# One-hot rows of 19 of 32 slot groups moved from ScalarE and VectorE to GpSimd

## What is computed

```python
x = x + _L0_xattn_ref(_layernorm(x), ctx_768, Wq, bq, Wk, bk, Wv, bv, Wo, bo)
x = x + _L0_ffn_ref(_layernorm(x), expert_embeddings, first_linear, second_linear)

# _L0_ffn_ref, the part that matters here
weights = _router(x, expert_embeddings)           # softmax over the top 2 of 8 experts
cap_ones = where(cumsum(ones, axis=0) <= 1024, ones, 0)
vals, idx = top_k((weights * cap_ones).T, 1024)   # per expert: which tokens it takes
tokens = x_flat[idx]
inter = relu(einsum('ech,eih->eci', tokens, first_linear))
out = einsum('eci,ehi->ech', inter, second_linear) * vals[:, :, None]
final = zeros.at[idx].add(out)
```

## Time and profile before

| | us |
|---|---|
| median of 3 runs | 1480.37 |
| lowest, highest | 1473.51, 1483.36 |
| the profiled execution | 1479.05 |
| its span, first to last instruction | 1477.3 |

### The profile page before, as it was taken

How to read it: one execution, slowest core, us unless ns; L and a number is a source line. 1 busy time by engine, 2 the same in 40 slices (tenths; PEclk the granted TensorE clock), 3 DMA queues, 4 the chain that set the end, 5 groups by cost and what they waited for, 6 DMA issues and landing times.

```text
span 1477.3 us, 30732 instructions
## 1 busy us (share of the span) xinstructions
PE 1338.2 (91%) x12330; PEld 786.1 (53%) x12330; DVE 997.5 (68%) x1998; ACT 814.1 (55%) x1344; POOL 702.3 (48%) x655
## 2 busy tenths in 40 slices
PE   7446999989999899997765999999999999999996
PEld 3334777766677667765444544444444444444442
DVE  6686888899889998899874644555454544555431
ACT  3556888877999889987554333425151433425110
POOL 2155877777777767776412424251413324251301
PEclk9767999999999999999787999999999999999998
DMA  7336798878878667786713665464646565474401
GB/s 220 101 92 136 191 228 216 216 175 208 196 210 193 176 157 177 186 216 146 197 61 116 180 157 158 131 178 119 182 136 157 159 160 163 132 169 118 105 15 43
DMA packets 321160, 231.78 MB, mean 157 GB/s; under 512 B 253481, under 2 KB 253865, under 8 KB 321018
## 3 DMA queue, kind: packets, MB, share of 16 engines
q1 hardware_dynamic: 305658, 179.17, 48.2%
q0 software_dynamic: 15360, 50.66, 11.5%
HBM read 121.87 MB, written 50.86 MB: 117 GB/s over the span
## 4 chain that ended last, share of the span: by engine, by line
PE 71%; DVE 16%; issue 4%; POOL 3%; ACT 3%; DMA 1%; SPq 1%; DVEq 0%; POOLq 0%; ACTq 0%
PE ps L1178 22%; PE ps L1164 22%; PE ps L1064 8%; PE ps L994 6%; PE ps L1045 4%; DVE ps L1409 2%; PE ps L1081 2%; PE ps L979 2%; DVE sd L1422 2%; DVE sm L1443 2%; DVE x L1465 1%; PE ps L1017 1%; PE ps L1059 1%; DVE xnT L1402 1%; PE ps L968 1%
## 5 line engine op out<-in xcount | busy, mean ns | idle before, releaser
L1164 PE MATMUL ps<-xT,w1s 128*128 128x512 f16 (+1 forms) x1632 | 335.9, 368 | 6.2 <-DVE xT L1708 5.4
L1178 PE MATMUL ps<-w2s,hT 128*128 128x512 f16 x1536 | 332.8, 379 | 0.0
L821 ACT ACTIVATE hT<-ps 128x512 f16<-128x512 f32 (+1 forms) x136 | 77.8, 572 | 359.6 <-PE ps L1164 359.6
L1164 PEld LDWEIGHTS ps<-xT,w1s 128*128 128x128 f16 x1632 | 160.4, 98 | 179.5 <-issue 5.8
L1178 PEld LDWEIGHTS ps<-w2s,hT 128*128 128x128 f16 x1536 | 150.3, 98 | 181.2
L994 PE MATMUL ps<-xnT,wqh 128*128 128x256 f16 x1536 | 202.1, 285 | 20.1 <-ACT partq L704 19.9
L542 POOL TENSOR_TENSOR sd<-sd,rr 128x1232 f32<-128x1232 f32 x64 | 144.2, 2253 | 145.6 <-ACT rr L722 145.6
L579 POOL DMA_INDIRECT out_dram<-ys,idx x64 | 71.7, 1120 | 278.4 <-DVE ys L1748 278.4
L1738 DVE SCALAR_TENSOR_TENSOR hT<-ps,hT 128x512 f16<-128x512 f32 (+1 forms) x136 | 88.6, 658 | 138.0 <-ACT hT L821 137.8
L1064 PE MATMUL ps<-woh,oT 128*128 128x512 f16 x768 | 179.9, 384 | 0.7 <-POOL oT L530 0.7
L994 PEld LDWEIGHTS ps<-xnT,wqh 128*128 128x128 f16 x1536 | 154.3, 102 | 47.7 <-ACT partq L704 21.5
(11 more groups left out here) (203 smaller groups left out, 2016.8 us busy)
## 6 DMA issues: line engine op xcount, KB each, us to landing
xt<-x SPq DMA_DIRECT2D x64, 256.0 KB, 3.4
xr<-x SPq DMA_DIRECT2D x64, 256.0 KB, 3.8
xrow_dram<-x SPq DMA_DIRECT2D x64, 256.0 KB, 3.7
out_dram<-x SPq DMA_DIRECT2D x64, 256.0 KB, 4.1
stage<-w1T SPq DMA_DIRECT2D x8, 2048.0 KB, 9.9
stage<-w2T SPq DMA_DIRECT2D x8, 2048.0 KB, 8.4
xs<-x SPq DMA_DIRECT2D x62, 256.0 KB, 3.9
wqf<-wq SPq DMA_DIRECT2D x1, 1024.0 KB, 7.1
```

The lines of the kernel that those rows point to most:

```text
L1164: ins = pe.matmul(hb[z][:, 0:wide], w1s[e % 2][:, a, k, ic * P:(ic + 1) * P], xT[:, 4 * b + k, cols], start=(k == 0 and i == 0), stop=(k = ...
L1178: ins = pe.matmul(yb[z][:, :], hT[:, a, k, s * P:(s + 1) * P], w2s[e % 2][:, b, k, :], start=(k == 0 and i == 0), stop=(k == 7 and i == 2))
```

## The change

One-hot rows of groups 0 to 15, 25, 27 and 29 are made on GpSimd, with DVE's form: compare and multiply in one instruction a row, four a group. ACT keeps 16, 18, 20, 22, 24, 26, 28 and 31, DVE keeps 17, 19, 21, 23 and 30. In the loop GpSimd makes half a group at the end of a beat, behind `p_lo`; groups 25, 27 and 29 stand behind its loop. PE waits for a semaphore of GpSimd's (`pickp`) for those groups.

```diff
-        vector_ones = lambda G: G >= 16 and G % 2 == 1 and G not in (29, 31) or G == 30
-        act_ones = [G for G in range(NG) if not vector_ones(G)]
+        vector_ones = lambda G: G in (17, 19, 21, 23, 30)
+        pool_ones = [G for G in range(NG) if G < 16 or G in (25, 27, 29)]
+        act_ones = [G for G in range(NG) if G not in pool_ones and not vector_ones(G)]
...
+            def onehot(G):
+
+                t0 = TG * G
+                R = span_of[t0]
+                j0 = t0 - r_span[R][0]
+                if G == 0:
+                    pool.wait_ge(S["own"], 2)
+                    pool.wait_ge(S["early"], 10)
+                if G >= 4:
+                    pool.wait_ge(S["inv"], G - 3)
+                pool.wait_ge(S["sx"], R + 1)
+                for j in range(TG):
+                    row = rowf[:, R % 2, j0 + j, :]
+                    n = (t0 + j) % TPB
+                    for k in range(2):
+                        ins = pool.tensor_scalar(pick[:, G % 4, j, k, :], iota[:, :], row[:, k:k + 1],
+                                                 local[:, n:n + 1], ALU.is_equal, ALU.mult)
+                    if j == TG - 1:
+                        ins.then_inc(S["pickp"], 1)
+                    yield
...
                 p_lo(h + 5)
-
+                for H in ones_at(h):
+                    if H < 16:
+                        ones = onehot(H)
+                steps(ones, 1)
+
+            for G in (25, 27, 29):
+                steps(onehot(G), 2)
             attention_done(pool)
...
                 for G in groups:
-                    if vector_ones(G):
+                    if G in pool_ones:
+                        pe.wait_ge(S["pickp"], pool_ones.index(G) + 1)
+                    elif vector_ones(G):
...
             value(25)
-            late_onehot(25)
             value(26)
             steps(last, 99)
             value(27)
-            late_onehot(27)
```

More of the change, by code:

```diff
@@ L54 @@
             "xlo hlo y gt gs")
-FROM_POOL = "made vz allmax chain normp qlo olo pz pn plo n2p w1r w2r"
+FROM_POOL = "pickp made vz allmax chain normp qlo olo pz pn plo n2p w1r w2r"
 class Count:
@@ L606, in gpsimd @@
             second = iter(())
+            ones = iter(())
             for h in range(-8, T):
@@ L768, in onehot @@
                     act.wait_ge(S["inv"], G - 3)
-                if G == 0:
-                    act.wait_ge(S["own"], 2)
-                    act.wait_ge(S["early"], 10)
                 for j in range(TG):
@@ L853, in scalar @@
                            ).then_inc(S["hi"], 1)
-            ones = iter(())
             for h in range(-8, TAIL):
@@ L858, in scalar @@
                 Q, part = divmod(h + 9, 2)
-                for H in ones_at(h):
-                    ones = onehot(H)
                 ln1_apply(h + 12)
@@ L866, in scalar @@
                 s_exp(h + 6)
-                steps(ones, 1)
                 r_scale(h + 5)
@@ L887, in scalar @@
                 t2_copy(h)
-                if h == 55:
-                    steps(ones, 4)
                 for H in ones_at(h):
@@ L903, in scalar @@
             second_exp(4)
-            steps(onehot(29), 4)
             w_hi(0, 1, 3)
@@ L1601, in ranking @@
                 if R >= 2:
-                    dve.wait_ge(S["pick"], TG * sum(TG * G < r_span[R - 2][1] for G in act_ones))
+                    by_act = TG * sum(TG * G < r_span[R - 2][1] for G in act_ones)
+                    if by_act:
+                        dve.wait_ge(S["pick"], by_act)
+                    dve.wait_ge(S["pickp"], sum(TG * G < r_span[R - 2][1] for G in pool_ones))
                 dve.wait_ge(S["v"], v.n)
```

## The result

The changed kernel takes **1516.51 us** (median of 4 runs, 1514.44 to 1520.53), beside 1481.86 for the kernel before (4 runs, 1473.51 to 1485.17). The ratio is 1.0236, 95% interval 1.0210 to 1.0261: slower by 34.7 us. The forecast was 1503.4, slower by 23. The time lies above the band of 1498 to 1509 that had half of the chance, and inside the outer range of 1490 to 1519. The sign, the place and the mechanism came as forecast. One term was half its true size, and a rival that I had nearly dismissed is present in small.

A forecast was written before the change was run, and what follows sets the result against it. PE was taken to pace regular beats, DVE the routing stretches. Stalls of 15.2 us in PE-paced beats plus 7.8 in routing ones make 23.0: 1480.4 + 23 = 1503.4 us, 8 in 10 from 1490 to 1519.

The forecast's parts named there:

- What bounds the kernel: PE sets the pace in regular beats of 9.44 us; DVE is the bound in the routing stretches.
- The new wait on PE: Each inversion waits for GpSimd's pair behind `p_lo`: 1.44 - 0.42 + 2 x 0.40 + 0.08 = 1.90 us, not draining.
- The price of one instruction: One GpSimd one-hot instruction on 128x128 was put at 0.40 us, between 0.21 and a cap of 0.70.
- How many pay: Of 16 inversions, eleven stall 1.90 us, eight of them in PE-paced beats; two stall 2.8 us, three nothing.
- What ACT's relief is worth: ACT loses some 1.3 us a beat, off the path; only `p_lo` gains, 0.42 us; nothing else counted.
- The routing stretches: Beats where DVE ranks beside usual work: five inversions in or at their edge cost together 7.8 us.
- The other half of the pair: Two instructions (0.8 us) between `p_lo` and `p_norm` in beat h fit GpSimd's idle time, perhaps not in routing stretches.
- groups 25, 27 and 29: Behind the loop, on idle GpSimd: they cost nothing, and the gain was priced at 0.
- A: Stall hidden where DVE is the bound; only eight PE-paced inversions pay, 15.2 us, 1495.6; chance 0.15.
- B: DVE held at the port shared with GpSimd, up to 1516, or a 0.70 us instruction, 1511 to 1512; chance 0.20.
- C: No loss: ACT's relief shortens routing stretches, 1476 at best; chance 0.07, of which 0.03 truly faster.
- D: PE's granted clock falls to 0.83 in all 32 beats, about 60 us more, 1563; chance 0.03.

The follow-up runs named there:

- experiment 3: Changed kernel with each one-hot pair a beat earlier (1496.50 us, ratio 1.0020), or with inversions of groups 0 to 14 a beat later (1495.45 us, ratio 0.9998).
- experiment 5: `four_late`: the changed kernel with all four one-hot instructions of a group behind the same `p_lo`; 1551.93 us (one run).
- experiment 2: Changed kernel with GpSimd's one-hot pair ahead of `p_lo` of the same beat instead of behind it; 1503.52 us, ratio 1.0055 to the kernel before.
- experiment 6: Kernel before with only groups 25, 27 and 29 moved to GpSimd, behind its loop; 1481.54 us, ratio 0.9992.

## Why the prediction was right, and where not

- **What bounds the kernel.** Right. PE paced the regular beats, and all that was added ahead of its inversion came out at its end (experiments 3 and 5).
- **The new wait on PE.** Right: the path through `q_hi`, `p_hi`, `p_lo` and the pair, no draining. `p_lo` gains 0.48 us, where I had capped it at 0.42 by the end of `q_lo`: it starts 1.02 us behind `o_mm` (441.60 - 440.58) instead of 1.50. The cap was misread, since `q_lo` comes sooner too and `p_lo` still waits for `p_hi`. Experiment 3 removes the loss by order alone, experiment 2 three quarters of it. That "every group pays again" is shown by the beats, which never catch up.
- **The price of one instruction.** This term was mis-sized. I took 0.40 us and capped it at 0.70; it is 0.79. I had bounded it by rows of arithmetic alone, and a 128-column product and sum does take 0.44, but no row held a comparison. The cap was the weak point: a larger instruction of another operation is no upper bound. With the Trainium skill, "GPSIMD Engine Reference", section 3.1 (1.8 cycles an element at best), and a fixed part of 0.2 I had estimated 0.39. For this form the measurement disagrees and decides. With 0.79 the stall by my formula is 1.44 - 0.42 + 1.57 + 0.08 = 2.67 us instead of 1.90; the rows show 2.56.
- **How many pay.** 15 inversions wait instead of 13: the dearer pair also reaches the two that had waited for the ranking. PE stood 1.60 and 1.20 us at these before (519.96 and 678.76), for DVE, and stands 1.97 and 1.76 now, so they add little. One of them I should not have put at nothing even at 0.40 us: before, `p_lo` ended at 678.19 and the inversion came at 678.76, 0.57 us later, and the pair with its semaphore wants 0.88. The eight in PE-paced beats were counted rightly.
- **The sum with the true price.** With 1.57 for the pair and both of these, my sum is 8 x 2.67 + 3 x (2.67 - 0.6) + (3.59 - 0.7) + (3.59 - 1.0) + (1.65 - 0.97) + (1.65 - 0.57) = 21.4 + 6.2 + 2.9 + 2.6 + 0.7 + 1.1, some 35 us, beside 34.7 measured. Here 3.59 is 1.94 + 1.57 + 0.08, 1.65 is 1.57 + 0.08, and 0.6, 0.7 and 1.0 are the prediction's. That it comes so close is partly luck: it leaves out two terms in the regular stretches, and gives more than was measured in the routing ones (next two points).
- **What ACT's relief is worth, and the clock.** I counted nothing for ACT in the regular beats, as PE waited for nothing there. Its weight loads waited 0.24 us a group for `x1T`, seven times, 1.7 us. With the clock's four falls of 1.6 us: 7 x 2.67 + 4 x 1.6 - 1.7 = 23.4 us for the regular stretches, measured 23.1.
- **The routing stretches.** I had 9.7 us with the eighth inversion; the true price makes it 16.1; 13.8 are measured, against one execution of before, whose unchanged code gives up to 5.0 us more in another (experiment 6). So the measured loss there is some 9 to 14 us. How much is hidden beside DVE in each place stays open.
- **The other half of the pair; groups 25, 27 and 29.** Right, nothing that can be measured (experiments 3 and 6). DVE's longest instructions did not grow: `put` 1956 ns, 2630 before, and `pick` 2532, 2535 before.
- **The rivals.** A fell: the routing stretches lost some 9 to 14 us. B had two halves. Its port half gave 1516, which is the time measured, but that is a coincidence: in experiment 3 the same instructions make no loss. The dearer instruction (1511 to 1512 at 0.70) was the cause, with a price beyond its bound. C fell: DVE-bound stretches gave nothing back. D I had at 0.03, for the whole of the time or not at all, with the argument that PE's mean share stays high. By my own sign, under 0.95 between 385 and 700 us, it did not come: the mean granted clock there is 0.96. But the clock does fall, for some 3 us behind seven of the 15 pauses, and PE's mean share over beats did not tell that.

## What to carry to other kernels

Work given to an idle engine is paid for where it stands in that engine's queue. Here the same two instructions cost 35 us behind `p_lo`, some 8 ahead of it and none that could be measured a beat earlier, so ask first which instruction waits for them and how late the one ahead already is. Where no row shows the operation itself, one from another class of arithmetic is no bound; leave room for twice, or measure it in an idle place first. And after an engine is relieved, look for what now meets on a shared resource, before counting the relief as a gain.

## What the runs showed of the hardware

- GpSimd, `tensor_scalar` on 128x128 f32 to f16: comparison and product with scalars from memory 0.79 us, with constants 0.64, comparison alone 0.64, product and sum 0.44 (means of three). The first with 64 columns instead of 128 is 0.65, with an f32 result 0.84. DVE does the first in 0.34.
- TensorE's granted clock was 1.00 in a pause of 2.40 us and fell behind it: 0.59 over 3 us behind the pause at 443.3, and not at all behind the one at 422. In all it fell behind 7 of the 15 pauses, 1.6 us lost each time in the regular stretches. With pauses of 3.47 to 4.35 us (`four_late`) it was down behind 14 of 15, in some already from within the pause. Filled pauses kept it at 1.00.
- `put` on DVE, started 0.33 us behind a `p_lo` on GpSimd, took 2.49 us instead of 0.48 and ended 0.28 us after it. The Trainium skill, "SBUF — State Buffer", section "SBUF: two separate sides", has a rule of the shared port held for a whole instruction. By that rule, the rows agree roughly: 0.28 us is less than the 0.41 that a `put` takes at its shortest, so the hold is not shown to the digit.
